# Third convolution: four groups of nodes in each spread operation and each accumulator bank, in place of two

## The reference

```python
t = h @ stn4_w + stn4_b
new_pseudo = jnp.clip(pseudo + t[col] - t[row], 0.0, 1.0)
basis2, idx2 = spline_basis(new_pseudo)
return spline_conv(x, row, col, basis2, idx2, conv_w, conv_b)

def spline_conv(x, row, col, basis, idx, W, b):
    z = jnp.einsum('ni,kio->nko', x, W).reshape(N * K, Fout)
    gathered = z[col[:, None] * K + idx]
    msg = jnp.einsum('es,eso->eo', basis, gathered)
    out = jax.ops.segment_sum(msg, row, num_segments=N)
    deg = jax.ops.segment_sum(jnp.ones_like(msg[:, 0]), row, num_segments=N)
    return out / jnp.maximum(deg, 1.0)[:, None] + b
```

## Time and profile before

| | us |
|---|---|
| median of three runs | 12598.79 |
| profiled execution, its own time | 12589.85 |
| its span, first to last instruction | 12588.1 |
| PE busy (matmul) | 7543.9 (60%) |
| DVE busy | 7405.1 (59%) |
| ACT busy | 2403.5 (19%) |
| POOL busy | 7822.8 (62%) |
| mean granted clock of TensorE | 0.798 of 2.4 GHz |

### The profile page before, as it was taken

One profiled execution on the slowest core, in us unless ns is written; L12 is line 12 of the kernel. 1 busy time (PEld: TensorE's weight loads), 2 busy tenths in 40 slices (PEclk: granted clock), 3 DMA queues, 4 the chain that ended last, 5 costly groups with the idle time before them and its releaser, 6 DMA issues. The chain is left out here.

```text
span 12588.1 us, 217168 instructions
## 1 busy us (share of the span) xinstructions
PE 7543.9 (60%) x58315; PEld 6771.0 (54%) x58315; DVE 7405.1 (59%) x17622; ACT 2403.5 (19%) x6396; POOL 7822.8 (62%) x7603
## 2 busy tenths in 40 slices
PE   0335777777366488888888445655565344444446
PEld 0334666666366477777777345555554244444443
DVE  4997666666588666666666257777777133333342
ACT  0001222222000033333333122222222000000001
POOL 0004777777344488888887088888885477777740
PEclk9998777777788799999999567777777577777775
DMA  0002000000811244444444234344343222222210
GB/s 23 0 0 94 3 3 3 3 3 3 19 28 28 43 94 94 94 93 94 93 93 91 9 56 61 61 62 62 62 62 47 33 58 56 55 58 58 54 49 5
DMA packets 1793503, 600.75 MB, mean 48 GB/s; under 512 B 1605562, under 2 KB 1736090, under 8 KB 1793207
## 3 DMA queue, kind: packets, MB, share of 16 engines
q1 hardware_dynamic: 1087784, 310.74, 13.3%
q0 software_dynamic: 252512, 268.68, 10.4%
q10 hardware_dynamic: 453168, 20.88, 3.0%
HBM read 424.44 MB, written 174.93 MB: 48 GB/s over the span
## 5 line engine op out<-in xcount | busy, mean ns | idle before, releaser
L1042 PE MATMUL c_acc<-c_spread_sb,c_basis_sb 128*125 128x256 f32 (+1 forms) x12544 | 2609.0, 380 | 1400.4 <-DVE c_basis_sb L956 1057.1
L1042 PEld LDWEIGHTS c_acc<-c_spread_sb,c_basis_sb 128*125 128x125 f32 x12544 | 2318.9, 237 | 1656.7 <-issue 1440.2
L1378 POOL DMA_INDIRECT at_ring<-gat_table,at_place x1568 | 1653.3, 1054 | 704.9 <-issue 704.9
L839 POOL DMA_INDIRECT c_ring<-hid_table,c_at x1568 | 1729.2, 1103 | 464.4 <-issue 462.7
L1081 ACT ACTIVATE c_sums<-c_acc 125x512 f32<-125x512 f32 (+1 forms) x3136 | 1537.1, 490 | 2489.0 <-PE c_acc L1042 2450.0
L545 POOL DMA_INDIRECT rec<-rk_rec,rk_place x1568 | 1587.2, 1012 | 534.7 <-issue 503.6
L839 POOL DMA_INDIRECT c_ring<-feat_table,c_at x1568 | 1594.8, 1017 | 464.4 <-issue 454.3
L1533 PE MATMUL at_acc_ps<-at_prod,ident 128*128 128x128 f32 x8036 | 1018.5, 295 | 1403.1 <-DVE at_prod L1479 1403.1
L1533 PEld LDWEIGHTS at_acc_ps<-at_prod,ident 128*128 128x128 f32 x8036 | 1009.4, 211 | 1412.1 <-issue 1412.1
L939 DVE TENSOR_TENSOR c_spread_sb<-c_mark,c_rin 128x512 f32<-128x512 f32 (+1 forms) x3136 | 1624.6, 553 | 0.0
L966 DVE TENSOR_SCALAR c_rel<-c_rin,first 128x16 f32<-128x16 f32 x392 | 102.5, 262 | 1577.7 <-DMA c_rin<-rows 961.7
(11 more groups left out here) (330 smaller groups left out, 10911.8 us busy)
## 6 DMA issues: line engine op xcount, KB each, us to landing
c_rin<-rows SPq DMA_DIRECT2D x3136, 42.0 KB
c_rin<-rows SPq DMA_DIRECT2D x3136, 20.0 KB
rows<-c_ring POOLq DMA_DIRECT2D x392, 128.0 KB
rows<-rk_blank SPq DMA_DIRECT2D x112, 252.0 KB
rows<-c_ring POOLq DMA_DIRECT2D x392, 72.0 KB
rows<-at_ring SPq DMA_DIRECT2D x196, 144.0 KB, 1.8
rec<-rk_rec,rk_place POOLq DMA_INDIRECT x1568
c_ring<-hid_table,c_at POOLq DMA_INDIRECT x1568
```

Of the source, the lines that this page charges most:

```text
L839: pool.indirect_dma_start(out=ring[:, u, j, :], out_offset=None, in_=table, in_offset=bass.IndirectOffsetOnAxis(ap=at[:, h, u, j:j + 1], a ...
L1042: last = pe.matmul(acc[pp % BANKS][:, (w % 2) * WN * feats:(w % 2 + 1) * WN * feats], basis[:, q, w, :, :].rearrange("p a b -> p (a b)"), ...
L1378: pool.indirect_dma_start(out=ring[:, u, j, :], out_offset=None, in_=d.gat_table, in_offset=bass.IndirectOffsetOnAxis(ap=place[:, u, j:j + ...
```

## The change

In the third convolution alone, one spread operation of DVE now makes four groups (512 elements in each partition) in place of two (256), a bank of PSUM takes four groups (512 columns), and ACT copies 512 columns at a time. `span` is the number of groups: 2 in the second convolution, as it was, and 4 in the third. So `pieces` falls from 8 to 4 in each half, and with it the counts of `spread_made`, `summed` and `taken`. Four of the eight places in DVE's chain where a spread operation stood have none now.

```diff
+    span = 2 if moved is None else 4
+    pieces = GW2 // span
-    pair = 2 * WN * feats
+    pair = span * WN * feats
...
+                        w = slice(k * span, k * span + span)
+                        dve.tensor_tensor(spread[:, q, w, :, :], bc(mark[:, q, w, :].unsqueeze(2), [P, span, feats, WN]),
+                                          bc(rin[:, q, w, 0:feats].unsqueeze(3), [P, span, feats, WN]), ALU.mult)\
                             .then_inc(spread_made, 1)
...
                 dve.tensor_reduce(tsrc[:, :, :], tsel[:, :, :, :].rearrange("p g r k -> p g k r"), X, ALU.add)\
                     .then_inc(seq, 1)
-                make_spread(1)
                 after_step(5)
                 dve.tensor_tensor(pos[:, :, :], pos[:, :, :], tsrc[:, :, :], ALU.subtract).then_inc(seq, 1)
-                make_spread(2)
+                make_spread(1)
                 after_step(6)
                 dve.tensor_scalar(pos[:, :, :], pos[:, :, :], 0.0, 1.0, ALU.max, ALU.min).then_inc(seq, 1)
-                make_spread(3)
                 after_step(7)
...
-                make_spread(4)
+                make_spread(2)
                 after_step(9)
...
-                make_spread(5)
                 after_step(10)
                 dve.tensor_scalar(three, three, 0.0, None, ALU.max).then_inc(seq, 1)
-                make_spread(6)
+                make_spread(3)
                 after_step(11)
                 make_plane(hat[:, :, :, :])
-                make_spread(7)
                 after_step(12)
                 make_basis(hat[:, :, :, :])
...
-                    if w % 2 == 0:
-                        pe.wait_ge(spread_made, (m + 2) * pieces + w // 2 + 1)
+                    if w % span == 0:
+                        pe.wait_ge(spread_made, (m + 2) * pieces + w // span + 1)
 
                         pe.wait_ge(taken, item * (2 * pieces) + pp + 1)
-                    last = pe.matmul(acc[pp % BANKS][:, (w % 2) * WN * feats:(w % 2 + 1) * WN * feats],
+                    last = pe.matmul(acc[pp % BANKS][:, (w % span) * WN * feats:(w % span + 1) * WN * feats],
...
                         act.activation(
+                            sums[:, :, pp * span * WN:(pp + 1) * span * WN].rearrange("p f (k n) -> p k f n", n=WN),
+                            acc[pp % BANKS][:, 0:pair].rearrange("p (k f n) -> p k f n", k=span, n=WN), ACT.Copy)\
                             .then_inc(taken, 1)
```

More of the change, by code:

```diff
@@ L797, in flow_conv @@
     cleared = sem(f"{name}_cleared")
-    pieces = GW2 // 2
+    span = 2 if moved is None else 4
+    pieces = GW2 // span
     loads = 16 * (GW2 if moved is None else GW2 + 1)
     steps = 4 if moved is None else 14
-    pair = 2 * WN * feats
+    pair = span * WN * feats
     with nc.Block() as block, ExitStack() as ctx:
@@ L937, in make_spread @@
                     for k in ks:
-                        w = slice(k * 2, k * 2 + 2)
-                        dve.tensor_tensor(spread[:, q, w, :, :], bc(mark[:, q, w, :].unsqueeze(2), [P, 2, feats, WN]),
-                                          bc(rin[:, q, w, 0:feats].unsqueeze(3), [P, 2, feats, WN]), ALU.mult)\
+                        w = slice(k * span, k * span + span)
+                        dve.tensor_tensor(spread[:, q, w, :, :], bc(mark[:, q, w, :].unsqueeze(2), [P, span, feats, WN]),
+                                          bc(rin[:, q, w, 0:feats].unsqueeze(3), [P, span, feats, WN]), ALU.mult)\
                             .then_inc(spread_made, 1)
@@ L1034, in body @@
                 for w in range(GW2):
-                    pp = q * pieces + w // 2
+                    pp = q * pieces + w // span
                     if w % G == 0:
                         pe.wait_ge(basis_made, m * 2 + w // G + 1)
-                    if w % 2 == 0:
-                        pe.wait_ge(spread_made, (m + 2) * pieces + w // 2 + 1)
+                    if w % span == 0:
+                        pe.wait_ge(spread_made, (m + 2) * pieces + w // span + 1)
                         pe.wait_ge(taken, item * (2 * pieces) + pp + 1)
-                    last = pe.matmul(acc[pp % BANKS][:, (w % 2) * WN * feats:(w % 2 + 1) * WN * feats],
+                    last = pe.matmul(acc[pp % BANKS][:, (w % span) * WN * feats:(w % span + 1) * WN * feats],
                                      basis[:, q, w, :, :].rearrange("p a b -> p (a b)"),
                                      spread[:, q, w, :, :].rearrange("p f n -> p (f n)"), start=True, stop=True)
-                    if w % 2:
+                    if w % span == span - 1:
                         last.then_inc(summed, 1)
@@ L1081, in _ @@
                         act.activation(
-                            sums[:, :, pp * 2 * WN:(pp + 1) * 2 * WN].rearrange("p f (k n) -> p k f n", n=WN),
-                            acc[pp % BANKS][:, 0:pair].rearrange("p (k f n) -> p k f n", k=2, n=WN), ACT.Copy)\
+                            sums[:, :, pp * span * WN:(pp + 1) * span * WN].rearrange("p f (k n) -> p k f n", n=WN),
+                            acc[pp % BANKS][:, 0:pair].rearrange("p (k f n) -> p k f n", k=span, n=WN), ACT.Copy)\
                             .then_inc(taken, 1)
```

## The result

The changed kernel takes 12643.35 us, the median of 7 runs (12626.13 to 12658.89), the kernel before 12592.42 us in 7 runs beside it: a ratio of 1.0039, 95% interval [1.0027, 1.0051]. It is slower by 51 us where +50 was forecast. That is only 0.4%, but the interval lies clear of 1. A second pair on another occasion gave 12633.75 us against 12583.97, a ratio of 1.004 [1.0026, 1.0053].

What follows compares the result with a forecast made beforehand. POOL's gathers were taken to bound the third convolution; +50 us on them, with DVE, ACT and the tail counted as nothing, added to the median 12598.79 us gave 12649 us. Range 12600 to 12690 us.

Steps and rivals of the forecast that it cites:

- What bounds: Third convolution: POOL's 1568 gathers and 392 stores set the pace, 24.5 us a block; SP could do 22.3.
- DVE, PE, ACT: Third convolution's other engines: DVE busy time 657 to 539 us, ACT 133 us less, PE's start nearly unmoved; hidden behind POOL.
- The gain in the body: DVE's chain per half block: 0.28 us less for each of 196 bodies, hidden in all but the last.
- The end of the stage: Tail after POOL's last store in the third convolution: between −1 and +0.2 us, counted as nothing.
- The gathers: POOL's gathers in the third convolution: held longer by long spread operations, +50 us taken, all reaching the end.
- random fall: First way for the gathers: falling at random on spread operations they lose 37 us now, 75 after; +37 us.
- o = 84: Second way, from the second convolution's gathers: o is the loss to all other DVE operations; 84 gives +49 us.
- As often and twice as long: Halved number, doubled length of spread operations: a gather meets one equally often, then waits twice as long.
- The phase: Gathers after the last spread operation would fall into basis: 39 us more if one body in four; range only.
- The exclusive lock: Skill's rule on the port pair DVE and GpSimd share: held for the whole instruction, so twice the length, twice the wait.
- The remark of the same page: Skill's probe saw tensor_tensor not stall a DMA's descriptor generation; by that the gathers' sum would be 0.
- the reading of the indices: About 0.1 us after its start a gather reads indices from SBUF; a DVE operation with two SBUF operands holds it up.

Runs made afterwards that it cites:

- e4_behind_plane: Changed kernel with its fourth spread operation moved from ahead of the plane operation to behind it, slow chip; 14924.43 us, 0.9838 of the kernel before.
- e1_banks: Kernel before with only the 512-column accumulators and ACT copies of the change, spread operations still 256, slow chip; 15089.43 us, ratio 0.993 to before.
- e5_banks_again: 512-column accumulators and ACT copies as in the change, spread operations of 256 as before, normal chip; 12591.04 us, ratio 1.0002 to the kernel before.
- b0_before: The kernel before, unchanged, profiled again on the normal chip; 12586.32 us.
- e10_psum_pairs: Mark and plane in PSUM in both convolutions, but spread in pairs (256) and accumulators of 256 as before the change, slow chip; 16671.95 us, 1.0979 of before.
- e3_mark_psum: Changed kernel with c_mark of the third convolution in PSUM, slow chip; 15084.89 us, 0.9938 of the kernel before.
- e9_mark_psum_again: Changed kernel with c_mark of the third convolution in PSUM, a repeat run on a slow chip; 15116.47 us, 0.9951 of the kernel before.
- e2_spread: Kernel before with only the change's spread operations of 512, accumulators and ACT copies still 256, slow chip; 15065.97 us, 0.9916 of before.
- e7_spread_again: Spread operations of 512 alone, accumulators and ACT copies of 256 as before, a repeat run on a slow chip; 15029.46 us, 0.991 of before.
- e8_1024: Changed kernel with two spread operations of 1024 a half block in place of four of 512, slow chip; 14699.36 us, 0.9678 of the kernel before.

## Why the prediction was right

*What bounds.* POOL, before and after: SP waits for its stores 87 and 86 times, and the gathers' sum and the stage grow by the same amount in both pairs (64.9 and 63.8 us; 46.2 and 46.4). Since the profiled executions differ by 69.0 us in one pair and 42.0 in the other, it is chance that the medians come within 1 us of the forecast.

*DVE, PE, ACT.* 688 ns was forecast for the long spread operation, 683 measured; 597 ns for ACT, 597 measured. The gain in the body was put at 0.28 us; from `c_rel` to the end of basis the median body is 9.17 us in place of 9.76, so 0.58 us were saved, twice as much. It is hidden in all but the last body either way. The accumulators cost nothing (1.0002).

*The end of the stage.* From the start of the last gather to the end of the last copy of `c_sums` it was 70.1 us, now 68.7: −1.4 where −1 to +0.2 was forecast, nothing against 50.

*The gathers.* By random fall 37 us were to become 75; by count over the trace 35.6 became 84.7 and 82.1. By the second convolution, o = 84 was taken for the other operations and measured at 121 − 36 = 85. The +49 us of that way is what the spread's share grew by (49.1 and 46.5). "As often and twice as long" holds: 7 to 9% more often and 2.2 times as long. Random fall with the most that a gather lost (0.28 and 0.55 us) gives 40 us and 78 us, so the growth of 2.3 times is the doubling and some phase; how much of each, nothing here separates.

*The phase.* This term, kept out of the sum, failed. After a wait for the last spread operation the next gather was to fall into basis, and basis to cost up to 39 us more. Basis fell by 19 and 29 us, and plane rose by 30 and 26. Half of the step is right: basis was slipped past by 159 gathers that started just at its start, and by 7 after the change. It left out the plane operation, which now starts 0.12 us behind a spread operation, itself has two SBUF operands, and stops the gathers first (143 in place of 45). The gather after one released by it starts 1.12 us later, about 0.1 us before the first basis operation ends, and so isn't held by the second either (8299.51 above; 124 bodies in place of 77 have a gather that runs over the start of the second). e4_behind_plane shows the same exchange the other way. With hat (+9 us) the operations that were not changed add 16 us in the first pair and nothing in the second.

*Two statements of the Trainium skill.* The exclusive lock of the Trainium skill's page "SBUF — State Buffer", section "SBUF: two separate sides", agrees with the rows here in one direction: a gather that starts in an operation with two SBUF operands waits for its end, however long it is, and not for one whose other operand is in PSUM. In the other direction it doesn't: with a gather running over the start of the second, two basis operations lose 0.06 us at most, not the rest of the gather. The measurement decides. The remark of the same page of the Trainium skill, section "Who interferes with whom", by which `tensor_tensor` doesn't stall descriptor generation, doesn't hold for these gathers: 0.54 us for one 512-element operation before, 0.47 at 8292.64. It does fit POOL's direct stores, which take no indices from SBUF: all 392 take 0.79 to 0.83 us, before and after. That points at the reading of the indices as what is held, as the prediction had it; no run took the indices away.

## What to carry to other kernels

Where GpSimd issues gathers at the pace of a stage, look at the spread of their durations: each that is longer than the shortest points, by its end, to the VectorE operation that held it. Merging small two-operand VectorE operations into longer ones can then cost more than it saves, as it did here with VectorE waiting for much of the stage; putting one of the two operands in PSUM takes the hold away and was worth 2.2% on the normal chip. Measure it where the kernel will run: on a slow chip the kernel with `c_mark` and `c_plane` in PSUM and pairs took 9.8% more, for a reason that is open. Where POOL set the pace, fewer instructions on the engines that wait were worth nothing.

## What the runs showed of the hardware that was not expected

The same kernel took 12584 us on one chip and 15174 and 15195 us on two others. e1_banks and e5_banks_again are one kernel on either kind of chip. Of the 2572 us between their profiled executions only 626 lie in the third convolution (3099 and 2473 us); the other three quarters lie in stages where nothing was tried. In the third convolution PE stands idle there without anything that the profile shows as the cause ("issue"), and SP hardly waits for POOL (three waits for stores, 17.5 us). PE's waits in e1_banks:

```profile
PE c_mix L1057 <- issue: 376.1, 299, 15.6
PE c_acc L1045 <- issue: 370.8, 145, 125.6
```

The longest, 125.6 us, is the start of the stage. On the normal chip b0_before shows 5.2 us for such waits:

```profile
PE c_acc L1042 <- issue: 5.2, 1, 5.2
```

Once POOL is through, e1_banks works off a block in 22.3 us, as SP does on the normal chip; beside POOL it takes 27 to 50 us, 35 on average. And there the order is turned round: the freer POOL runs, the later the others come. In the order of the time over which the gathers are spread:

| run | to before | first to last gather, us | first gather to last copy, us |
|---|---|---|---|
| e10_psum_pairs | 1.0979 | 2308 | 3614 |
| e3_mark_psum | 0.9938 | 2384 | 3061 |
| e1_banks | 0.993 | 2388 | 3099 |
| e9_mark_psum_again | 0.9951 | 2395 | 2998 |
| e2_spread | 0.9916 | 2418 | 2992 |
| e4_behind_plane | 0.9838 | 2431 | 2921 |
| e7_spread_again | 0.991 | 2440 | 2927 |
| e8_1024 | 0.9678 | 2559 | 2630 |

In e8_1024 the last copy ends 71 us after the last gather starts, as on the normal chip, so there POOL is the pace again. On these chips, then, spread operations of 1024 made the kernel faster than those of 512 (0.9678 and 0.991 on one chip), though its gathers take longer; on the normal chip longer ones cost time. The number of instructions by itself doesn't explain it: e10_psum_pairs has as many for DVE (17622) and ACT (6396) as the kernel before, and takes 1477 us more. Whether it is the fetching of instructions beside POOL's DMAs or something else no run here tells; it stays open.
